# Attention and gated feed-forward on one core: scores taken singly between two halves of the product with v

## What is computed

```python
def _layernorm(x, axis=-1, eps=1e-05):
    m = jnp.mean(x, axis=axis, keepdims=True)
    v = jnp.var(x, axis=axis, keepdims=True)
    return (x - m) / jnp.sqrt(v + eps)
...
    # q: layernorm(x), (8, 512, 1024); k and v: both ctx_512, (8, 512, 256)
    qh = q.reshape(B, S, KV, G, D).transpose(0, 2, 3, 1, 4)
    kh = k.reshape(B, S, KV, D).transpose(0, 2, 1, 3)
    vh = v.reshape(B, S, KV, D).transpose(0, 2, 1, 3)
    scores = jnp.einsum('bkgsd,bktd->bkgst', qh, kh) / scale
    weights = jax.nn.softmax(scores, axis=-1)
    out = jnp.einsum('bkgst,bktd->bkgsd', weights, vh)
...
    x = x + _L0_xattn_ref(_layernorm(x, axis=-1), ctx_512, ctx_512)
    x = x + _L0_ffn_ref(_layernorm(x, axis=-1), ...)
```

## Time and profile before

| | before |
|---|---|
| median of three runs | 1045.58 us |
| the profiled execution's own time | 1049.05 us |
| its span | 1047.3 us |
| TensorE busy | 952.5 us |
| VectorE busy | 913.2 us |
| GpSimd busy | 799.4 us |
| ScalarE busy | 733.5 us |
| TensorE's granted clock, mean | 0.986 |

### The profile page before, as it was taken

One profiled execution on the slowest core, in us unless ns is written; L12 is line 12 of the kernel. 1 busy time (PEld: TensorE's weight loads), 2 busy tenths in 40 slices (PEclk: granted clock), 3 DMA queues, 4 the chain that ended last, 5 costly groups with the idle time before them and its releaser, 6 DMA issues.

```text
span 1047.3 us, 24586 instructions
## 1 busy us (share of the span) xinstructions
PE 952.5 (91%) x9518; PEld 374.1 (36%) x9518; DVE 913.2 (87%) x1106; ACT 733.5 (70%) x1301; POOL 799.4 (76%) x454
## 2 busy tenths in 40 slices
PE   4779999999999999999999999999999997999996
PEld 3222222222222222222222222222222225777773
DVE  6969999999999999999999999998888874888976
ACT  5457777777777777777777777777777775544440
POOL 7259988888889999999999999998999995322210
PEclk9989999999999999999999999999999998999998
DMA  7765676767676767676767576756556742666423
GB/s 241 198 148 110 158 156 160 157 155 162 148 162 154 168 140 176 140 170 141 178 142 175 131 182 134 186 107 155 108 121 152 161 109 98 216 228 219 163 101 161
DMA packets 319875, 164.18 MB, mean 157 GB/s; under 512 B 182216, under 2 KB 307240, under 8 KB 319760
## 3 DMA queue, kind: packets, MB, share of 16 engines
q1 hardware_dynamic: 319456, 161.76, 62.7%
q0 software_dynamic: 304, 0.85, 0.4%
HBM read 107.58 MB, written 54.53 MB: 155 GB/s over the span
## 4 chain that ended last, share of the span: by engine, by line
PE 66%; DVE 16%; ACT 9%; issue 7%; POOL 2%; DMA 0%; DVEq 0%; SPq 0%; POOLq 0%; ACTq 0%
PE psum L596 19%; PE psum L610 17%; ACT probs L870 8%; DVE row_max L933 6%; PE psum L558 6%; PE psum L623 5%; PE psum L633 5%; PE psum L741 5%; PE psum L719 4%; PE psum L584 3%; DVE probs L1145 2%; DVE prod_mem L991 2%; PE psum L707 1%; DVE row_max L924 1%; PE psum L641 1%
## 5 line engine op out<-in xcount | busy, mean ns | idle before, releaser
L870 ACT ACTIVATE probs<-psum 128x512 f32<-128x512 f32 x1024 | 562.1, 597 | 155.1 <-PE psum L596 135.7
L933 DVE TENSOR_REDUCE row_max<-psum 128x4 f32<-128x2048 f32 x248 | 566.3, 2283 | 69.8 <-PE psum L558 66.3
L596 PE MATMUL psum<-q_stack,k_stack 97*32 97x512 f16 x4096 | 347.7, 388 | 48.7 <-ACT probs L870 35.8
L357 POOL TENSOR_TENSOR sums<-probs 128x2048 f32<-128x2048 f32 x63 | 286.9, 4553 | 61.3 <-PE psum L633 60.2
L367 POOL TENSOR_TENSOR sums<-probs 128x2048 f32<-128x2048 f32 x63 | 287.4, 4563 | 21.5 <-ACT probs L870 21.5
L610 PE MATMUL psum<-probs,v_in 128*32 128x512 f32 x2048 | 267.4, 598 | 0.0
L596 PEld LDWEIGHTS psum<-q_stack,k_stack 97*32 97x32 f16 x4096 | 91.8, 94 | 300.0 <-ACT probs L870 213.4
L558 PE MATMUL psum<-high_mem 32*128 32x512 f16 x992 | 98.0, 385 | 5.6 <-DVE row_max L933 5.2
L334 POOL TENSOR_TENSOR o_all<-o_all,o_t 128x512 f32<-128x512 f32 x64 | 81.4, 1272 | 9.2
L610 PEld LDWEIGHTS psum<-probs,v_in 128*32 128x32 f32 x2048 | 63.2, 111 | 55.6 <-issue 21.3
L341 POOL TENSOR_SCALAR var_eps<-mv 128x1 f32<-128x1 f32 x32 | 9.2, 288 | 89.0 <-DVE mv L1019 88.4
(11 more groups left out here) (119 smaller groups left out, 769.0 us busy)
## 6 DMA issues: line engine op xcount, KB each, us to landing
q_stack<-q_split SPq DMA_DIRECT2D x192, 128.0 KB, 3.5
xa<-in_x_dram SPq DMA_DIRECT2D x32, 512.0 KB, 4.5
o_all<-in_x_dram SPq DMA_DIRECT2D x256, 64.0 KB, 2.4
x_attended<-o_all SPq DMA_DIRECT2D x64, 256.0 KB, 4.6
out_dram<-probs SPq DMA_DIRECT2D x32, 512.0 KB, 2.9
q_split<-prod_mem SPq DMA_DIRECT2D x15, 1024.0 KB, 5.6
xa<-x_attended SPq DMA_DIRECT2D x16, 512.0 KB, 4.5
probs<-x_attended SPq DMA_DIRECT2D x16, 512.0 KB, 4.6
```

The costliest lines, as they stand in the source:

```text
L357: pool.tensor_tensor(sums[:, (2 * u - 1) % SUMS], probs[:, (u - 1) % 2, 2], probs[:, (u - 1) % 2, 3], ALU.add).then_inc(back_done, 1)
L596: last = pe.matmul(st_ps[row:row + D, bank_of["score", u, n], :], k_stack[:, u % SLOTS, t * P + row:t * P + row + D], q_stack[:, u % SLOTS ...
L870: act.activation(probs[:, s, keys, g, :], st_ps[:, bank_of["score", u, n], :], ACT.Exp, scale=EXP_SCALE).then_inc(exped, 1)
L933: dve.reduce_max(row_max[:, u % 2, t:G * ST:ST], s_ps[:], AX.X).then_inc(reduced, 1)
```

## The change

The tables BEGIN and MIDST become one table PLACES, with five numbers a quarter. The product with v is issued in two halves of two groups each; the semaphore `pv_done` is raised by the second. Scores between the first and second number stand ahead of the first half, up to the third number between the halves, up to the fourth behind the second half, and the rest behind the first denominators (on t = 2 also behind the row maxima). Odd units have 5, 4, 4, 3 scores a quarter, even ones 4, 5, 3, 4 as before. The last unit has all scores of a quarter ahead of the product, as before. The planner of the banks follows the new order, and so does ScalarE.

```diff
-            BEGIN = ((0, 4, 9, 12, NSC), (0, 5, 10, 13, NSC))
-            MIDST = ((2, 6, 11, 14), (2, 7, 12, 15))
+            PLACES = (((0, 2, 3, 4, 4), (4, 6, 7, 8, 9), (9, 10, 11, 11, 12), (12, 14, 15, NSC, NSC)),
+                      ((0, 2, 3, 4, 5), (5, 7, 8, 9, 9), (9, 11, 12, 12, 13), (13, 14, 15, 15, NSC)))
...
-                    now += scores[:half]
+                    now += scores(0, 3)
                     if t == 2 and live(u + 1):
                         now.append(("max", u + 1, 0))
-                    now += scores[half:]
                     if t == (ST - 1 if u % 2 == 1 else 2) and live(u - 1):
                         now.append(("den", u - 1, 0))
+                    now += scores(3, 4)
...
-                def gather(u, t):
+                def gather(u, t, half):
...
-                    for g in range(G):
+                    for g in range(2 * half, 2 * half + 2):
                         last = pe.matmul(o_ps[g * D:(g + 1) * D, :], v_in[:, u % 2, t, :],
                                          probs[:, u % 2, t, g, :], start=(t == 0), stop=(t == ST - 1))
-                    last.then_inc(pv_done, 1)
+                    if half == 1:
+                        last.then_inc(pv_done, 1)
...
+                        if t > 0 and live(u):
+                            gather(u, t - 1, 0)
+                        if 0 <= u < UNITS - 1:
+                            score_keys(u, places[1], places[2])
+                        if t == 0 and live(u - 1):
+                            gather(u - 1, ST - 1, 1)
+                        if t > 0 and live(u):
+                            gather(u, t - 1, 1)
                         if t == 0 and live(u - 2) and u % 2 == 0 and u < UNITS:
                             last_denominators(u - 2)
+                        if 0 <= u < UNITS - 1:
+                            score_keys(u, places[2], places[3])
                         if t == 2 and 0 < u + 1 < UNITS:
                             turn_max(u + 1)
-                        if 0 <= u < UNITS - 1:
-                            score_keys(u, MIDST[u % 2][t], BEGIN[u % 2][t + 1])
                         if t == (ST - 1 if u % 2 == 1 else 2) and live(u - 1) and live(u):
                             first_denominators(u - 1)
+                        if 0 <= u < UNITS - 1:
+                            score_keys(u, places[3], places[4])
```

More of the change, by code:

```diff
@@ L205, in xattn_ffn @@
                 for t in range(ST):
-                    scores = [("score", u, n) for n in range(BEGIN[u % 2][t], BEGIN[u % 2][t + 1])] if live(u) else []
-                    half = MIDST[u % 2][t] - BEGIN[u % 2][t]
+                    scores = lambda first, last: [("score", u, n) for n in range(
+                        PLACES[u % 2][t][first], PLACES[u % 2][t][last])] if live(u) else []
                     now = []
@@ L677, in _ @@
                             fold_constants()
-                        if live(u):
-                            score_keys(u, BEGIN[u % 2][t], MIDST[u % 2][t])
+                        places = PLACES[u % 2][t]
+                        if 0 <= u < UNITS - 1:
+                            score_keys(u, places[0], places[1])
                         if u == UNITS - 1:
-                            score_keys(u, MIDST[u % 2][t], BEGIN[u % 2][t + 1])
+                            score_keys(u, places[0], places[4])
                         if t == ST - 1 and live(u - 1) and live(u) and u % 2 == 0:
                             last_denominators(u - 1)
[L684 to L688, removed]
+                        if t == 0 and live(u - 1):
+                            gather(u - 1, ST - 1, 0)
+                        if t > 0 and live(u):
+                            gather(u, t - 1, 0)
+                        if 0 <= u < UNITS - 1:
+                            score_keys(u, places[1], places[2])
+                        if t == 0 and live(u - 1):
+                            gather(u - 1, ST - 1, 1)
+                        if t > 0 and live(u):
+                            gather(u, t - 1, 1)
                         if t == 0 and live(u - 2) and u % 2 == 0 and u < UNITS:
                             last_denominators(u - 2)
+                        if 0 <= u < UNITS - 1:
+                            score_keys(u, places[2], places[3])
                         if t == 2 and 0 < u + 1 < UNITS:
                             turn_max(u + 1)
-                        if 0 <= u < UNITS - 1:
-                            score_keys(u, MIDST[u % 2][t], BEGIN[u % 2][t + 1])
                         if t == (ST - 1 if u % 2 == 1 else 2) and live(u - 1) and live(u):
                             first_denominators(u - 1)
+                        if 0 <= u < UNITS - 1:
+                            score_keys(u, places[3], places[4])
                         if u == UNITS - 1 and t == ST - 1:
@@ L859, in _ @@
                             s = u % 2
-                            for n in range(BEGIN[u % 2][t], BEGIN[u % 2][t + 1]):
+                            for n in range(PLACES[u % 2][t][0], PLACES[u % 2][t][4]):
                                 keys, g = n // G, n % G
@@ L864, in _ @@
                                     wait(act, front_done if keys < ST // 2 else back_done, u - 1)
-                                if n == MIDST[u % 2][2] and live(u + 1):
+                                if n == PLACES[u % 2][2][3] and live(u + 1):
                                     make_shift(u + 1)
```

## The result

The changed kernel takes 1097.16 us (median of four runs, 1095.35 to 1098.94), the kernel before 1045.57 (median of four). The ratio is 1.049, with a 95% interval of 1.046 to 1.052. One execution of e3 (1739.20 us) and one of the kernel before (1346.07 us) were slow and enter no ratio, and since e3's profile fell in its slow one, e3b is the same kernel executed once more for a profile.

The account below looks back on a forecast made before the run. TensorE was taken as the bound (busy 91%; ScalarE and VectorE wait for it). Eight quarters summed to 27.84 for 25.87 us, +1.97 a pair over 31.5 pairs, +62 us: 1108 us, between 1060 and 1160.

Parts of the forecast that it names:

- E0: Quarter t = 0 of even units, L558 to L558: later exponential 15 and held half make it 3.75 us, +0.73.
- Rival (a): TensorE's array takes matmuls strictly in order, so halves and score follow each other: +4.61 a pair, 1191 us, chance 0.05.
- Rival (b): In the product with v, a half costs half, 0.43 us: 25.82 a pair, 1044 us, chance 0.05.
- The held second half: In TensorE's queue the second half stands behind the third score's wait; strips B idle 0.74 to 0.80 us.
- Rival (c): Strips B are not held by the third score's wait, halves cost nothing: -0.93 a pair, 1016 us, chance 0.10.
- O2: Quarter t = 2 of odd units: held second half and one more score make it 3.98 us, +1.00.
- O1: Quarter t = 1 of odd units: four scores for five, the saving eaten by strips B: 3.55 us, -0.09.
- E1's gain: Quarter t = 1 of even units: early first exponential, release 0.51 after the product's start: 3.26 us, -0.30.
- The denominators: First denominators ahead of the last score: t = 3 of odd units 2.79, t = 2 of even unchanged, E3 +0.76.
- E3: Quarter t = 3 of even units: exponential 12 behind the normalisation, score 14 released 0.9 later: 3.78 us, +0.76.
- O0: Quarter t = 0 of odd units: only the third score moves, 3.61 us, +0.06.
- VectorE's floor of 2.98 for O3: Quarter t = 3 of odd units: VectorE needs 0.52, 2.29 and 0.17 between L558 groups, holding 2.79 at 2.98.

Follow-up runs that it names:

- e3: Kernel before with one score between the product's halves, nothing else of the change: 1064.41 us, ratio 1.017.
- e3b: Same kernel as e3 (kernel before, one score between the halves), executed again for an undisturbed profile: single run 1066.89 us.
- e6: Kernel before with one edit: at t = 0 of even units the second score, its bank free early, stands between the halves: 1045.71 us, ratio 1.000.
- e1: Order of the kernel before, with the product issued as two halves right behind each other, nothing between: 1045.45 us, ratio 0.9996.
- e5: Changed kernel with the product parted into three groups and one, in place of two and two: 1096.19 us, ratio 1.048 to the kernel before.
- e2: Changed kernel with nothing between the halves; score counts and denominators' place stay changed: 1058.84 us, ratio 1.013 to the kernel before.
- e7: Kernel before with 5, 4, 4, 3 scores in odd units, halves right behind each other, no other edit: 1046.73 us, ratio 1.000.
- e9: Kernel before with one edit, the third score between the halves at t = 1 of even units: 1045.16 us, ratio 1.0005.
- e8: Kernel before with only the first denominators moved ahead of the last score (t = 3 odd, t = 2 even units): 1059.67 us, ratio 1.013.
- e4: Changed kernel with the first denominators back behind the last score: 1091.78 us, ratio 1.046 to the kernel before.

## Why the prediction was right, and where it was not

```profile
L596 PE MATMUL psum<-q_stack,k_stack 97*32 97x512 f16 x4096 | 347.7, 388 | 48.7 <-ACT probs L870 35.8
```

Eight records of 0.594 us add up to 4.75 us and lie within 1.03. The first four, one of each group, all start at 432.4. E0 of after and e6 show the same for halves of a score and of a product, which run side by side (in e6 both start at 469.28) though the order in the program is another. Rival (a), by which the array takes matmuls strictly in order, does not hold here: in E0 two matmuls of the score start at 467.00 ahead of the two that come before them in the program, at 467.35. What rival (a) made of it, halves that follow each other on the whole array, is refuted by e1 (1045.45 us), which would be some 200 us slower. The semaphore of a score is raised by the last of its four matmuls, on strips B. In e6 strips B finish their half of score 1 at 469.66 (469.28 + 0.38), this matmul among them, and the exponential starts only at 470.58, 0.44 behind the start of the other half at 470.14. So the score counted as finished there only when all its strips were through.

**A half is not half the time: right.** The second half of E0 takes two passes, from 467.22 to 468.1, the 0.86 of a whole product, and in e5 one group behind the wait costs as much as two. Rival (b) rested on the opposite.

**The held second half: right as a mechanism.** e6 takes the wait away and e1 the score, and neither costs anything; e3 adds a score with a wait alone and costs 18 us. With the other two edits in place it is worth 1.39 a pair (after less e2), without them 0.69 (e3b less before). Rival (c) had it that strips B would not be held; in E0 they are, for 0.74.

**The place where it costs: partly wrong.** The step that failed is O2, in its cause: "Now: first half to 2.22, score 11 released at 2.16, second half on B 2.37 to 3.22 ... at 3.98. That is +1.00". The short steps at its end can be read from the trace of before: the transpose of the maxima starts at 436.96, 0.10 behind the 0.86 of the product, the score at 437.29, 0.33 later, and L558 at 437.62, 0.11 behind the 0.22 of the score. In the changed kernel the times do follow this path, up to the last score, which starts 0.20 behind the maxima and not 0.33 (462.34 and 462.14), so that O2 is 3.88. But the working left out a second path nearly as long: the maxima's bank waits for exponential 10 and the last score's for exponential 11, and the parts start later behind a short O1. By these alone, with no half held, O2 is 3.79 (e7, e2), where the same working gave 3.21 (the expectation of e2); the held half adds 0.09. O1 is the other way: there the count wins 0.66 and the held half takes 0.59 back. That the score given away was eaten by strips B in O1 was right.

**E1's gain: right in size, wrong in cause.** The text put it on the early release in E1. e9 has that release (0.47 behind the product's start) and E1 is no shorter, since its last score waits for an exponential.

**The denominators: right for E3, not for E0.** E3's late exponential 12 costs 0.22 alone (e8) and 0.75 where a second half stands behind it (after against e4). E0's later exponential 15 costs 0.23 alone (e8), and the working of E0 started from it. But e3b has E0 at 3.77 without it: the score between the halves is released 1.51 behind L558 in e3b and after alike (448.88 - 447.37 and 466.99 - 465.48), whether the product starts at 0.77 or at 1.00. The row of e3b is

```profile
448.88 0.10 PEld L596 LDWEIGHTS psum<-q_stack,k_stack 97*32 97x32 f16 x4 [0.62 <-ACT probs L882]
```

The held half alone gives all of E0's loss.

**O0: forecast 3.61, measured 3.50.** With the denominators where they were it is 3.63 (e3b, e4): there the parts start 0.48 behind L558 (449.06 - 448.58 in e4), 0.15 after VectorE has taken the denominators from the bank (448.20 to 448.91). In the changed kernel they start at 0.32. The working had not followed the parts.

**VectorE's floor of 2.98 for O3: wrong.** O3 took 2.81. In O3 of after the reduction starts 0.45 behind L558 (463.12 - 462.67), takes 2.29, and the next L558 follows 0.07 behind its end. The 0.52 was read in one quarter (434.64 to 435.16), in which VectorE had been idle for 0.82; why it is longer there no row shows. The 0.17 was not VectorE's either: L558 at 437.62 stood right behind a score that started at 437.29. This changed nothing in the sum, since the prediction gave the 0.19 back in E0.

**The size, 62 us for 49 of span.** 25 pairs at +1.87 are 47 us, where +1.97 was forecast: 2.5 us too much. The last pairs, some five, have no tile work left and grow from 24.12 to 24.81, by 0.69; the prediction gave them +1.97 too, 6 us too much. The first pair of the stage did not grow at all (33.50 and 33.43), 2 us more. The last 2 us were not traced.

**The signs that the prediction named.** The pair is 27.74 for 27.8. The second half starts 1.03 behind the first in O1 (457.61 - 456.58) and 1.04 in O2 (461.18 - 460.14), as said, but 0.74 in E0. VectorE waits 97 us for L558 where about 120 was given. ScalarE's idle time ahead of the third score of E0 is 0.36 and not 0.1 (467.79, from the same trace):

```profile
467.79 0.60 ACT L879 ACTIVATE probs<-psum 128x512 f32<-128x512 f32 x1 [0.36 <-PE psum L596]
```

## What to carry to other kernels

Work that runs side by side on strips of the array should be split only where nothing that waits comes between the pieces. Here each piece took as long as the whole (0.86 us), and a wait in between left the other strips empty for its length. Before moving an instruction within a queue, list which bank each one behind it takes and which other engine's instruction frees it. Moving the fifth score by one quarter won nothing, since there the maxima and the last score came to wait one exponential longer; moving it by two won 0.6%. Single edits of an order don't add up: here three edits of +0.01, +0.48 and +0.69 a pair together gave +1.87.

## What was not expected of the hardware

In E0 of after and in e6, matmuls that come later in the program started ahead of earlier ones, on strips that were free. In E0 of after two matmuls of the score do so at 467.00, ahead of its other two at 467.35. In e6 two start at 469.28 and their other two at 470.14, behind both passes of the half product. But the score counted as finished only with its slowest strip: in e6 0.9 us lie between the end of strips B (469.66) and the exponential (470.58). A score on half-free strips therefore gained its reader nothing here.
